# Transposing the attention heads' exponentials: on TensorE, or on VectorE with transfers through memory

## The reference, cut to what matters

```python
x = _layernorm(x + _L0_gnn_ref(x, adj, ...))   # graph attention, ELU
x = _layernorm(x + _L1_gnn_ref(x, adj, ...))   # 3 x (attention, layernorm, 256-1024-256 GELU network, layernorm)
x = _layernorm(x + _L2_gnn_ref(x, adj, ...))   # graph attention, the 16 largest weights of a row kept, ELU
x = _layernorm(x + _L3_gnn_ref(x, adj, ...))   # 8 heads of 32 columns, masked softmax, ReLU, projection

# _L3_gnn_ref
q, k, v = heads(x @ Wq), heads(x @ Wk), heads(x @ Wv)
scores = jnp.einsum('bhnd,bhmd->bhnm', q, k) / sqrt_dk
scores = jnp.where(mask, scores, -jnp.inf)
attn = jax.nn.softmax(scores, axis=-1)
out = jnp.einsum('bhnm,bhmd->bhnd', attn, v)
return jax.nn.relu(out.transpose(0, 2, 1, 3).reshape(b, n, d)) @ Wo
```

## Time and profile before

| | us |
|---|---|
| Time, median of 3 runs (lowest, highest) | 3469.51 (3466.64, 3474.24) |
| Time of the profiled execution | 3471.65 |
| Its span, first to last instruction | 3469.9 |
| Granted TensorE clock, share of full speed, mean | 0.976 |
| Opening, about | 185 |
| Seven loop passes, two half-batches each, about | 2920 |
| Closing, about | 364 |
| Bytes moved by transfers | 40.4 MB |

### The profile page before, as it was taken

The page is one execution under the profiler, slowest core; times in us unless marked ns, Lnnn a source line. Parts: engine busy times, 40 slices in busy tenths (PEclk is TensorE's granted clock), DMA queues, the critical chain, the costliest instruction groups (busy, mean ns, idle before and its releaser), DMA issues.

```text
span 3469.9 us, 59779 instructions
## 1 busy us (share of the span) xinstructions
PE 3168.8 (91%) x18688; PEld 2526.4 (73%) x18688; DVE 2490.8 (72%) x8197; ACT 2143.3 (62%) x4255; POOL 739.3 (21%) x1049
## 2 busy tenths in 40 slices
PE   5699999999999999999998999999999999999976
PEld 4577777777777777777777778677777777778664
DVE  4567787777767777687767867777687767777765
ACT  3356656665666756656666666757656666566634
POOL 1221221222221221221222221221221212221210
PEclk8899999999999999999999999999999999999989
DMA  6000000000000000000000000000000000000000
GB/s 153 0 1 13 7 13 8 2 12 7 13 8 7 7 7 13 8 13 8 1 13 8 13 7 7 7 8 13 7 13 8 1 13 7 13 8 1 1 7 7
DMA packets 39413, 40.40 MB, mean 12 GB/s; under 512 B 6704, under 2 KB 37680, under 8 KB 39088
## 3 DMA queue, kind: packets, MB, share of 16 engines
q1 hardware_dynamic: 30640, 27.94, 2.8%
q0 software_dynamic: 8448, 8.39, 1.7%
HBM read 36.33 MB, written 8.39 MB: 13 GB/s over the span
## 4 chain that ended last, share of the span: by engine, by line
issue 42%; PE 39%; DVE 9%; POOL 9%; ACT 1%; POOLq 0%; DMA 0%; DVEq 0%; SPq 0%; ACTq 0%
PE work L1223 8%; PE acc L1237 7%; PE acc L1199 5%; POOL rstd L501 4%; PE acc L1272 3%; PE acc L1284 3%; PE work L1284 3%; PE acc L1303 3%; POOL R L509 2%; POOL R L513 2%; PE work L1252 2%; PE work L1155 1%; DVE T L673 1%; PE work L1184 1%; DVE T L690 1%
## 5 line engine op out<-in xcount | busy, mean ns | idle before, releaser
L501 POOL TENSOR_TENSOR rstd<-var_eps,minus_half 128x2 f32<-128x2 f32 x320 | 226.2, 707 | 2578.2 <-DVE var_eps L781 2578.2
L1223 PE MATMUL work<-XT,w_sb 128*128 128x256 f32 x3072 | 732.5, 384 | 31.5 <-DVE XT L829 16.1
L1237 PE MATMUL acc<-w_sb,gT 128*128 128x256 f32 x3072 | 720.1, 380 | 0.0
L1223 PEld LDWEIGHTS work<-XT,w_sb 128*128 128x128 f32 x3072 | 559.5, 190 | 161.9 <-ACT gT L1038 41.5
L1237 PEld LDWEIGHTS acc<-w_sb,gT 128*128 128x128 f32 x3072 | 575.1, 190 | 96.9 <-issue 22.8
L1038 ACT ACTIVATE gT<-work,b_sb 128x256 f32<-128x256 f32 x768 | 343.2, 471 | 212.4 <-PE work L1223 206.8
L1199 PE MATMUL acc<-X,PT 128*128 128x256 f32 x1536 | 368.2, 395 | 3.4 <-ACT PT L1006 0.9
L1199 PEld LDWEIGHTS acc<-X,PT 128*128 128x128 f32 x1536 | 295.4, 197 | 76.9 <-issue 25.1
L1056 ACT ACTIVATE T<-T,head_min 128x512 f32<-128x512 f32 x256 | 182.3, 713 | 117.7 <-DVE head_min L882 117.1
L772 DVE BATCH_NORM_STATS2 stats<-R 128x6 f32<-128x256 f32 x640 | 240.9, 418 | 11.0
L1199 PE MATMUL acc<-V,PT 128*128 128x256 f32 x1024 | 237.3, 385 | 4.5 <-ACT PT L1006 3.4
(11 more groups left out here) (151 smaller groups left out, 5771.6 us busy)
## 6 DMA issues: line engine op xcount, KB each, us to landing
HX<-in_x SPq DMA_DIRECT2D x16, 512.0 KB, 3.9
pos<-in_adj POOLq DMA_DIRECT2D x16, 512.0 KB, 5.6
out<-X SPq DMA_DIRECT2D x32, 256.0 KB, 2.1
w_sb<-in_L_gnn_W SPq DMA_DIRECT2D x6, 1024.0 KB, 9.5
awr_sb<-in_L_gnn_attn_w SPq DMA_DIRECT2D x3, 256.0 KB, 8.2
g_sb<-in_L_gnn_g SPq DMA_DIRECT2D x6, 128.0 KB, 6.9
c_sb<-in_L_gnn_beta SPq DMA_DIRECT2D x3, 128.0 KB, 4.4
gT<-in_L_gnn_b SPq DMA_DIRECT2D x3, 128.0 KB, 6.0
```

The lines of the kernel that those rows point to most:

```text
L501: pool.tensor_tensor(rstd[s][:, half_rows(half)], var_eps[s][:, half_rows(half)], minus_half[:], ALU.pow)\
L1223: last = pe.matmul(u.bank[:, 0:HN], w1_sb[:, l, c, f * P:(f + 1) * P], XT[s][:, c, half * HN:(half + 1) * HN], start=(c == 0), stop=(c == ...
L1237: last = pe.matmul(acc[s][half][:, i, :], gT[s][:, f, i * P:(i + 1) * P], w2_sb[:, l, f, :], start=(f == 0 and i == 0), stop=(f == FC - 1) ...
```

## The change

The exponentials of a tile are transposed in 32x32 blocks by VectorE ("bt", two tiles for each pair), which leaves every block in the right columns but on the wrong group of 32 partitions. SyncE writes a pair's two tiles to a scratch tensor in device memory, in four transfers of 32 partitions ("mw", 8 transfers of 128 KB for a quad), and reads each pair back in one transfer of 512 KB ("mr") with all blocks in place. Pair 0 is turned into the slot's `HX`, pair 1 into a new buffer that both slots share; they come back into `gT` and `PT2`. TensorE's transposes and both engines' copies of them go. The next batch's x is loaded into `HX` after the last quad is sent. The loops are written out in Python, so waits compare with constants. `mark()` goes. `HALF` is a new order, of which the part around the heads is shown.

```diff
     HALF = [
...
+        ("ending", "L3", "ex0 ex1 ex2 ex3 sq0 sr0"), ("middle", "L1.1", "bc zs0"), ("ending", "L3", "mr1 v1"),
+        ("middle", "L1.0", "xa0"), ("ending", "L3", "bt0 bt1"), ("middle", "L1.1", "mx0"), ("middle", "L1.0", "xa1"),
...
+        ("ending", "L3", "bt6 bt7 pv0 pc0 sq4 sr4 mw3 ex14 ex15"), ("middle", "L1.1", "f102 f103"),
+        ("ending", "L3", "rr0 bt8 bt9 ex16"), ("middle", "L1.1", "f200"), ("ending", "L3", "sq5 ex17 ex18 ex19"),
...
+        ("middle", "L1.1", "f112 f203"), ("middle", "L1.2", "sx0"), ("ending", "L3", "pv1 sq6 sr6 pc1 bt12 bt13"),
+        ("middle", "L1.1", "f113 f210"), ("ending", "L3", "mr2"), ("middle", "L1.1", "f211"), ("ending", "L3", "sq7"),
+        ("middle", "L1.1", "ha1"), ("ending", "L3", "mw4 ex24 ex25 sr7"), ("middle", "L1.1", "xsum1 xa0 xa1"),
+        ("ending", "L3", "bt14 bt15 mr3"), ("middle", "L1.1", "f212 xnorm1"), ("ending", "L3", "hn0 rr1 mw5 mr4"),
+        ("middle", "L1.2", "sx1"), ("middle", "L1.1", "f213"),
+        ("ending", "L3", "pv2 ex26 ex27 mr5 ex28 pc2 ex29 mw6 ex30 rb0 ex31 mw7"), ("middle", "L1.2", "zs0 zs1 bc"),
+        ("ending", "L3", "rb1 proj0 hn2"), ("middle", "L1.2", "exp0 exp1 mx0 mx1"), ("ending", "L3", "ysum0"),
+        ("middle", "L1.2", "pT0 pT1"), ("ending", "L3", "hn1 mr6 pv3 mr7 norm0 load"), ("middle", "L1.2", "pT2 pT3"),
+        ("ending", "L3", "ysum1 norm1"), ("starting", "L0", "masks"), ("ending", "L3", "proj1"),
+        ("starting", "L0", "xT"), ("middle", "L1.2", "agg0 sum0 agg1"), ("ending", "L3", "store0"),
+        ("starting", "L0", "v0"), ("middle", "L1.2", "norm0"), ("ending", "L3", "store1"),
     ]
...
+        turned_tail = sb("turned_tail", [P, HPC, D])
+        passing = nc.dram_tensor("passing", [SLOTS, NQ, 2, P, 2 * N], F32, kind="Internal").ap()
...
+        def moved_units(s, pair):
+            where = gT[s][:].rearrange("p f n -> p (f n)") if pair == 0 else PT2[:].rearrange("p r t n -> p (r t n)")
+            return where.rearrange("p (i n) -> p i n", i=HT)
+        def head_weights(s, r, j):
+            return moved_units(s, r // 2).rearrange("p i (a r t n) -> p r t (i a) n", a=HPC, r=2, t=NT)[:, r % 2, j]
+        def turned_units(s, pair):
+            return HX[s][:] if pair == 0 else turned_tail[:]
...
-                sp.wait_ge(kept.sems[s], kept.value(it, "L2", NT - 1))
+                sp.wait_ge(sent_away[0].sems[s], sent_away[0].value(it, f"q{NQ - 1}", 16 * HPC - 1))
                 hold(sp, "sync")
                 load_x(s, it.next())
...
+            def send_away(q):
+                def stage(s, it, key):
+                    for pair in range(2):
+                        sp.wait_ge(turned.sems[s], turned.value(it, "heads", HPC * q + 2 * pair + 1))
+                        hold(sp, "sync")
+                        there = passing[s, q, pair].rearrange("(g j) (a n) -> a j g n", g=HPC, a=HPC)
+                        for a in range(HPC):
+                            sp.dma_start(there[a], turned_units(s, pair)[a * DK:(a + 1) * DK]).then_inc(sent_away[pair].sems[s], 16)
+                return stage
+            def bring(q):
+                m, half, i = QUADS[q]
+                def stage(s, it, key):
+                    if i == 0 and q:
+                        outputs = HeadUse(s, it, 0, f"outputs {q // 2 - 1}")
+                        sp.wait_ge(outputs.filled, outputs.filled_at)
+                        hold(sp, "sync")
+                    for pair in range(2):
+                        sp.wait_ge(sent_away[pair].sems[s], sent_away[pair].value(it, f"q{q}", 16 * HPC - 1))
+                        hold(sp, "sync")
+                        sp.dma_start(moved_units(s, pair)[:, i], passing[s, q, pair]).then_inc(brought.sems[s], 16)
+                return stage
...
-            with sp.Fori(0, PAIRS - 1) as it:
+            for it in range(PAIRS - 1):
                 walk(it, to_a, stages)
                 walk(it + 1, to_b, stages)
...
-            def mark():
-                at = next(places)
-                dve.memset(marked[:, at:at + 1], 0.0)
...
+            def blocks_turned(q, pair):
+                def stage(s, it, key):
+                    if q:
+                        dve.wait_ge(sent_away[pair].sems[s], sent_away[pair].value(it, f"q{q - 1}", 16 * HPC - 1))
+                        hold(dve)
+                    for r in range(2):
+                        n = HPC * q + 2 * pair + r
+                        dve.wait_ge(exp_done.sems[s], exp_done.value(it, "heads", n))
+                        dve.transpose(turned_units(s, pair).rearrange("p g (r t j) -> p r g t j", r=2, t=NT)[:, r],
+                                      score_tile(s, n).rearrange("p (t g j) -> p g t j", t=NT, g=HPC))\
+                            .then_inc(turned.sems[s], 1)
+                return stage
...
-                    for r in range(HPC - 2, HPC):
-                        copied = HeadUse(s, it, place_of(q, r), f"pT {q}")
-                        pe.wait_ge(copied.evacuated, copied.done)
+                    pe.wait_ge(brought.sems[s], brought.value(it, f"q{2 * g + 1}", 16 * 2 - 1))
```

73 lines of the change are left out of this document (17 added, 56 removed), and 79 rows, old and new, of the table HALF.

## The result

The changed kernel takes 3508.0 us (3505.2 to 3513.2, 4 runs) against 3469.2 us (4 runs of before beside it): ratio 1.0111, 95% interval 1.0098 to 1.0123. It is slower by 39 us where I forecast 105 us less, and it lies outside the range. The profiled execution has a span of 3511.5 us and a mean granted clock of 0.945 (before 3469.9 and 0.976).

What follows compares the result with a forecast made beforehand. TensorE was taken to bound the kernel, VectorE becoming the fuller engine in the heads' stretch after the change. 3471.65 - 117 (heads' stretch) - 8 (loops) + 18 (last batch) = 3365 us; 8-in-10 range 3235 to 3490.

Steps and rivals of the forecast that it cites:

- all of the change's work lies in the first of these stretches: Only the 108 us where the ending batch's heads run beside the middle batch's L1.1 were taken to change.
- the term of 7.8 us per half-batch: Heads' stretch: VectorE's 90.2 us of work at 90% busy gives 100.2 us instead of 108; 15 times, 117 us.
- the loops' 8: Loops written out: TensorE's idle time at six loop returns, 8.4 us in sum, goes; gain 8 us (0 to 18).
- the last batch alone: Closing batch, where TensorE waits for VectorE: slower quads plus the last quad's round trip, +18 us (0 to 30).
- a quarter of the saving: Ahead of L1.2's broadcast, about a quarter of the saving becomes a wait for VectorE's chain; counted within the 7.8 us.
- Transposes: VectorE's 32 block transposes per half-batch, 128x512 f32, were taken at 0.69 us each, 22.1 us.
- VectorE's share: In the heads' stretch VectorE becomes the fuller engine, up from 74% busy to 90%.
- TensorE's busy time: Sign of being right: TensorE busy near 182 us per half-batch.
- Traffic: Scratch writes and reads: 268 MB, 27% of 16 engines' span, at no cost on the path in the steady state.
- the slower rival of the single buffer's round trip: A quad's round trip through the single buffer, 11.3 us, bounds the heads; 3623 us, chance 0.12.
- Late tiles: Rival: read-back reaches each batch's last product 4.4 us late, in 16 batches; 70 us more, 3435 us, chance 0.17.
- a granted clock clearly below the 0.98: Sign of being wrong: a TensorE with more idle time could get a lower clock.

Runs made afterwards that it cites:

- e8: Changed kernel with one order edit: GpSimd's affine step of L1.2 (ha0, ha1) moved earlier, away from L1.0's score products on VectorE; 3438.4 us, ratio 0.9899.
- e19: e8 with eight unused GpSimd products, which no other engine waits for, in the moved step's old place; 3511.1 us.
- e13: Separate kernel: six VectorE instruction kinds alone, then beside GpSimd products; product with sum 2.85 to 6.47 us, normalize 2.67 to 6.03, other four unchanged.
- e1: Kernel before, with only its loops written out; 3468.6 us, ratio 0.9984.
- e15: e8 with each of VectorE's 512 transposes cut to 32 columns, waits and transfers kept; 3429.2 us.
- e17: e8 without the transfers through memory, waits for them turned into waits for the transposes; 3415.4 us.
- e10: e8 with 44 unused TensorE transposes added ahead of L1.2's bc (broadcast of row scores); 3450.3 us.
- e14: e8 with ScalarE's copy of the third group's outputs behind the last exponentials, and two short VectorE steps behind L1.2's score products; 3441.3 us.
- e18: e14 with VectorE's last two transpose steps of each batch replaced by four tiny memsets that don't wait for the exponentials; 3432.0 us.
- e6: Changed kernel with VectorE's last two transpose steps and the two short steps behind them moved after the next layer's scores; 3604.7 us.
- e12: e11 with the end of the heads' stretch reordered on TensorE, VectorE and ScalarE, the last group's output product and projection coming later; 3584.7 us.
- e4: Changed kernel without its transfers through memory, the output product waiting for the turned tiles instead; 3490.8 us.
- e3: Changed kernel with unused TensorE transposes filling two waits, 44 ahead of L1.2's bc and 18 ahead of L1.0's; 3495.6 us.
- e11: e8 with two more GpSimd steps moved, ha1 of L1.1 ahead of xsum0 and xa0 ahead of xsum1; 3434.5 us, interval 0.9875 to 0.9911.

## Why the prediction was wrong

The forecast fails by 143 us, in two parts of about the same size.

**The step that failed first is one that isn't in the sum.** I wrote that "all of the change's work lies in the first of these stretches", cut the heads' stretch and left the rest of the half-batch as it was. I costed transposes, transfers, loops and waits, but not the new order of the other stages: I compared neither GpSimd's list nor what each of its steps would now lie beside. That is 70 us: shown by e8 (the step moved away, 3508 to 3438) and e19 (its mere work put back, 3438 to 3511), with the mechanism measured alone in e13. Without it the change is faster than before, so this step is also what turned the sign. The trace of before had it in plain sight: the same form (L673 T<-HX) takes 0.93 us in 17 of 256 places there, where GpSimd's X<-X,beta runs beside it. The Trainium skill, "SBUF — State Buffer", section "Who interferes with whom", has the rule: a VectorE instruction with two inputs in SBUF contends with a GpSimd instruction that reads SBUF, one in a two-port mode does too, and one with at most one input in SBUF outside these modes does not. Five of e13's six kinds agree with it as they stand. The sixth, normalize, has one input in SBUF; it agrees if it ran in a two-port mode, which the page says this kind of instruction can enter and no run here shows. The page also says that the loser is fully blocked for the other's whole instruction; by e13 a pair of the two starts every 0.86 us, less than the 0.35 + 0.68 us from start to start that they take when alone, so part of each runs beside the other, and the measurement decides.

**The second is the term of 7.8 us per half-batch.** I made it from VectorE's work divided by a share of 90%. With the collision gone (e8) the stretch ahead of the heads takes 124.6 us as before, the heads' stretch 75.8 for 77.8, and with the few us behind bc the whole half-batch is 3.8 us shorter (204.8 for 208.6; of these e1's loops are 0.7), not 7.8. Up to the last projection of the middle I had forecast 125 us less (15 x 7.8 and the loops' 8) and e8's trace has 59 less: 66 us are missing. The other 7 are the last batch alone (below). Together they are the 73 between e8 and the forecast.

The form of the term was wrong, not only its size: 13.4 us less work for VectorE change the half-batch by 0.02 us (e15), so a share of VectorE's is no measure of it. Nor is it the round trip (e17), and the clock given back brings nothing (e10). The gap ahead of L1.2's bc stays a suspect. In e8's heads' stretch TensorE is idle 12.8 of 75.8 us, 5.8 of them in this place, and every way that I tried to shorten it left the half-batch where it was (e14, e18, gap 5.0 and 4.4 us) or made it longer (e6, e12), but none closed it without another loss. So what sets 204.8 us stays open; that it is the waits along the layers' own chains is a guess. I had seen this chain and called it a part of the 7.8, a quarter of the saving; it is the larger for it that the earlier trace rows show TensorE's old transposes as nearly the only thing that filled it.

**By its other steps.** Transposes: 0.69 us, right. VectorE's share: 66.5 of 77.8 us, 86% where I took 90% (of a stretch cut longer, 108 us). TensorE's busy time: 187.0 us per half-batch where I named 182, and 184.5 in e8. Traffic: 29.8% of the engines' span, near the 27% and what the queue carried before. The transfers are hidden in the steady state, right (e4, e17); the slower rival of the single buffer's round trip didn't come, VectorE waits 8 us in all for it. Late tiles: pv waits 38.6 us for the read-back in the whole run, about half of that rival's 70, but removing it (e4) changes no half-batch. Loops: 8 forecast, 6 measured. The last batch alone: it took 25 us more (169.4 to 194.0) where I took 18, 12 of them up to its own first output projection (158.7 to 171.0) and 12 behind it (10.6 to 23.1). Most of the second part is the round trip, which pv3 waits for near the end:

```profile
3498.85 0.64 PE L1295 MATMUL acc<-gT,V 128*32 128x256 f32 x2 [8.45 <-DMA PT<-passing]
```

The clock: I named "a granted clock clearly below the 0.98" as a sign of error, and it came (0.945), but given back it was worth 12 us (e3).

The best complete versions measured are e11 and e8: 3434.5 and 3438.4 us, 1% faster than before and 2% faster than after, three and one moved entries of GpSimd's away from it.

## What to carry to other kernels

When a change comes with a new order, list for each engine which steps now run at the same time as which, GpSimd's too, and look in the old trace for a form whose duration has two values: the slow one shows who its bad neighbour is. Work that nobody waits for can still cost 2% of a kernel, through the one instruction that it slows on the way to a busy engine's next task. Don't turn relief into time by a busy share: take a good part of the suspected load away in one run. Here 13.4 us less of it left the period where it was to 0.02 us, so this load didn't set it.
